# An audio tower in three phases: first layers of every batch, 32 experts as one line, last layers, with h and x kept in DRAM between them

## The reference

```python
hq = jnp.einsum('bqe,he->bqh', Q, W1q)          # 16 hidden features
hk = jnp.einsum('bke,he->bkh', K, W1k)
hid = jnp.tanh(hq[:, :, None, :] + hk[:, None, :, :] + b1)
est = jnp.einsum('bqkh,h->bqk', hid, W2[0]) + b2[0]
attn = jax.nn.softmax(scores + est, axis=-1)    # scores = Q K^T / sqrt(128)
return jnp.einsum('bqk,bke->bqe', attn, V)
```

## Time and profile before

| | |
|---|---|
| median of three runs | 5201.93 us (5199.91 to 5202.93) |
| the profiled execution's own time | 5203.53 us |
| its span, first to last instruction | 5201.7 us, 84447 instructions |
| TensorE busy | 4439.2 us, 85% of the span |
| ScalarE, VectorE, GpSimd busy | 2955.1, 2858.5, 705.4 us |
| mean granted TensorE clock | 0.910 |

### The profile page before, as it was taken

The page is one execution under the profiler, slowest core; times in us unless marked ns, Lnnn a source line. Parts: engine busy times, 40 slices in busy tenths (PEclk is TensorE's granted clock), DMA queues, the critical chain, the costliest instruction groups (busy, mean ns, idle before and its releaser), DMA issues.

```text
span 5201.7 us, 84447 instructions
## 1 busy us (share of the span) xinstructions
PE 4439.2 (85%) x24924; PEld 2449.2 (47%) x24924; DVE 2858.5 (55%) x6651; ACT 2955.1 (57%) x6370; POOL 705.4 (14%) x477
## 2 busy tenths in 40 slices
PE   4599997898659999789865999978985699997998
PEld 3344443466434444346643444434663344443566
DVE  5577773234457778223445777822344577772244
ACT  1177875754217777574421877856441277775644
POOL 0112221000021222100002122210000122221000
PEclk8699998999669999899966999989996699998999
DMA  2133320000113332000012333200001332320000
GB/s 92 20 46 49 54 34 32 3 27 9 52 23 44 47 54 34 32 8 22 11 49 28 42 45 54 34 32 9 21 13 48 37 42 42 47 34 32 13 17 16
DMA packets 97459, 175.25 MB, mean 34 GB/s; under 512 B 18400, under 2 KB 75152, under 8 KB 96272
## 3 DMA queue, kind: packets, MB, share of 16 engines
q1 hardware_dynamic: 97040, 170.00, 18.6%
HBM read 94.13 MB, written 1.53 MB: 18 GB/s over the span
## 4 chain that ended last, share of the span: by engine, by line
issue 49%; PE 43%; DVE 3%; POOL 1%; POOLq 1%; DMA 1%; DVEq 1%; ACT 1%; SPq 0%; ACTq 0%
PE ps L809 10%; PE ps L845 10%; PE ps L819 9%; PE ps L879 3%; PE ps L888 3%; PE ps L800 2%; PE ps L906 2%; DVE peaks L1548 2%; POOL rstd L545 1%; DMA k_stack<-parts 1%; PE ps L651 1%; PE ps L869 1%; PE ps L911 1%; DVE xn L1392 1%; PE ps L828 1%
## 5 line engine op out<-in xcount | busy, mean ns | idle before, releaser
L1548 DVE TENSOR_REDUCE peaks<-ps 128x1 f32<-128x748 f32 (+1 forms) x1536 | 1403.3, 933 | 505.1 <-PE ps L819 480.3
L1197 ACT ACTIVATE masked<-ps 128x384 f32<-128x384 f32 (+3 forms) x1536 | 679.8, 485 | 195.8 <-PE ps L809 181.9
L1197 ACT ACTIVATE probs<-ps 128x384 f32<-128x384 f32 (+1 forms) x1536 | 661.8, 484 | 93.7 <-PE ps L809 92.9
L545 POOL TENSOR_TENSOR rstd<-var,minus_half 128x6 f32<-128x6 f32 x104 | 138.3, 1330 | 3268.8 <-DVE var L1388 3268.8
L819 PE MATMUL ps<-k_stack,q_stack 96*128 96x374 bf16 (+1 forms) x1536 | 405.7, 349 | 113.8 <-DMA k_stack<-parts 87.4
L809 PE MATMUL ps<-shared 98*128 98x384 bf16 (+3 forms) x1536 | 440.1, 327 | 14.0 <-ACT probs L1197 6.8
L809 PE MATMUL ps<-q_stack,k_stack 98*128 98x384 bf16 (+3 forms) x1536 | 451.6, 330 | 0.5
L1449 DVE TENSOR_REDUCE top<-ps 128x1 f32<-128x128 f32 (+4 forms) x240 | 151.5, 631 | 426.2 <-PEq L715 354.1
L819 PE MATMUL ps<-shared 96*128 96x374 bf16 (+1 forms) x1536 | 372.2, 323 | 5.9 <-DVE peaks L1548 4.9
L1140 ACT ACTIVATE probs<-ps,neg_top 128x128 f32<-128x128 f32 (+4 forms) x240 | 152.9, 640 | 300.4 <-DVE neg_top L1457 246.8
L809 PEld LDWEIGHTS ps<-shared 98*128 98x128 bf16 (+1 forms) x1536 | 145.5, 103 | 353.4 <-ACT masked L1197 140.5
(11 more groups left out here) (276 smaller groups left out, 7794.3 us busy)
## 6 DMA issues: line engine op xcount, KB each, us to landing
shared<-parts SPq DMA_DIRECT2D x192, 187.0 KB, 9.2
wr<-in_l SPq DMA_DIRECT2D x32, 580.5 KB, 3.6
q_stack<-parts SPq DMA_DIRECT2D x96, 187.0 KB, 8.1
k_stack<-parts SPq DMA_DIRECT2D x96, 187.0 KB, 10.1
wts<-in_l SPq DMA_DIRECT2D x32, 514.5 KB, 3.5
shared<-in_tv SPq DMA_DIRECT2D x4, 4096.0 KB, 13.1
wrow<-in_l_rows SPq DMA_DIRECT2D x32, 320.0 KB, 4.1
wts<-in_l SPq DMA_DIRECT2D x32, 257.5 KB, 2.6
```

The lines of the kernel that those rows point to most:

```text
L545: pool.tensor_tensor(rstd[:, :], var[:, :], minus_half[:, :], ALU.pow).then_inc(S["rstd_ready"], 1)
L1197: act.activation(probs_ring(u)[0:m, 0:hi - lo], src[0:m, 0:hi - lo], ACT.Exp, scale=float(HD) ** -0.5).then_inc(S["ring_done"], 1)
L1548: v.tensor_reduce(peaks[0:m, g, j, head:head + 1], src[0:m, :, 0:T // 2], XY, ALU.max)\
```

## The change

The loop `batch` is split in three. The loop `front` does stages 1 and 2 for all four batches. Then one `experts()` without a loop does 32 experts as one pipeline (stages e = -1 to 32), those of batch 3 first (its xn, xT_, h and gates are still on the chip), then of batches 0, 1 and 2. The loop `tail` does stages 4 and 5 for all four. Between the phases h, xn, xT_ and the gates of a batch lie in DRAM tensors (`saved`): `spill` writes them at the end of each front, the pipeline loads those of the next batch in the midst of the last experts of the one before, `spill_merged` writes the merged h, and `load_hn` reads it for the tail into the new tile `hn`. The next x is loaded while the front before it still computes its gate; `tv` is loaded once. The store of the output is waited for only where h is written again (`out_free`).

In the additive attention the products of the projection weights are formed once at the start (`fold_ready`, `fold_done`: W1q Wq, W1k Wk, and Wk^T Wq), so that one set of products from xT_ gives the hidden parts and the scaled queries, and the keys are xT_ itself; hqb is made in two parts. The tanh ring has eight buffers in place of four. ScalarE's order is now tanh of tile u with the exponential of tile u - 1 after the fifth of them; the last tile has 14 tanh in place of 16. VectorE copies both halves of the turned probabilities. TensorE weighs tile u after the seventh tanh product of tile u + 2. ScalarE loads the table of exp at the head of a tail.

The diff, cut to its core:

```diff
+RUN = B * E
+STAGES = (B - 1,) + tuple(range(B - 1))
+def batch_of(x):
+    return STAGES[x // E]
+def first_of_stage(x):
+    return 0 < x < RUN and x % E == 0
...
-def additive_groups():
-    return [4 * (i % 4) + i // 4 for i in range(P // 8)]
+def additive_groups(u):
+    groups = min(P, T - u * P + 7) // 8
+    order = [4 * (i % 4) + i // 4 for i in range(P // 8)]
+    return [(g, g % 4 == 3 or g == groups - 1) for g in order if g < groups]
+ADDITIVE = [additive_groups(u) for u in range(NT)]
+AHEAD = 5
+BETWEEN = 7
+def tanh_order():
+    for u in range(NT):
+        for i, (g, _) in enumerate(ADDITIVE[u]):
+            yield "tanh", u, g
+            if u and i == AHEAD - 1:
+                yield "exp", u - 1, None
+    yield "exp", NT - 1, None
...
+            .rearrange("p (t d) -> p t d", t=NT)
+        saved = {name: nc.dram_tensor("saved_" + name, (B, P, width), F32).ap()
+                 for name, width in (("h", TP), ("xn", TP), ("xT", TP), ("gates", E * NT))}
...
-            return hid[:, i % 4, :] if i % 4 < 2 else masked[:, i % 4 - 2, :]
+            return (hid[:, 0, :], hid[:, 1, :], masked[:, 0, :], masked[:, 1, :], flat(x1), flat(att), flat(y),
+                    merged[:, 0:TP])[i % 8]
...
+            def spill(b, following=None):
+                sp.wait_ge(S["h_ready"], n.take("h_ready"))
+                sp.dma_start(saved["h"][b, :, :], flat(h)).then_inc(S["h_spilled"], 16)
+                if following is not None:
+                    load_x(following)
+                sp.wait_ge(S["front_done"], n.take("front_done"))
+                sp.dma_start(saved["xn"][b, :, :], flat(xn)).then_inc(S["front_spilled"], 16)
+                sp.dma_start(saved["xT"][b, :, :], xT_).then_inc(S["front_spilled"], 16)
+                sp.dma_start(saved["gates"][b, :, :], flat(gates)).then_inc(S["front_spilled"], 16)
+                sp.wait_ge(S["h_spilled"], n.take("h_spilled", 16))
+                sp.sem_inc(S["h_free"], 1)
+                sp.wait_ge(S["front_spilled"], n.take("front_spilled", 48))
+                sp.sem_inc(S["front_free"], 1)
+            def spill_merged(b):
+                sp.wait_ge(S["merged"], n.take("merged"))
+                sp.dma_start(saved["h"][b, :, :], flat(h)).then_inc(S["merged_spilled"], 16)
+                sp.wait_ge(S["merged_spilled"], n.take("merged_spilled", 16))
...
+                            if first_of_stage(x + 1):
+                                sp.dma_start(xT_, saved["xT"][batch_of(x + 1), :, :]).then_inc(S["xt_loaded"], 16)
+                            if first_of_stage(e - 1):
+                                spill_merged(batch_of(e - 2))
+                                sp.dma_start(flat(h), saved["h"][batch_of(e - 1), :, :]).then_inc(S["h_loaded"], 16)
+                                sp.dma_start(flat(gates), saved["gates"][batch_of(e - 1), :, :])\
+                                    .then_inc(S["h_loaded"], 16)
...
+                            if first_of_stage(e):
+                                sp.wait_ge(S["base_ready"], n.now("base_ready"))
+                                sp.dma_start(flat(xn), saved["xn"][batch_of(e), :, :]).then_inc(S["base_loaded"], 16)
...
-            with n.loop(sp, "batch", B, S["loop_entered"]) as b:
-                sp.wait_ge(S["x_free"], n.take("x_free"))
-                sp.dma_start(xT[:, 0:T_IN], A["xT"][b, :, :]).then_inc(S["x_loaded"], 16)
-                sp.dma_start(tv[:, :, :], A["tv"]).then_inc(S["tasks_loaded"], 16)
-                load_wq(0)
-                load_wr(0)
-                experts()
+            load_x(0)
+            sp.dma_start(tv[:, :, :], A["tv"]).then_inc(S["tasks_loaded"], 16)
+            load_wq(0)
+            load_wr(0)
+            with n.loop(sp, "front", B - 1, S["loop_entered"]) as b:
+                spill(b, b + 1)
+            spill(B - 1)
+            experts()
+            def tail(b, following=None):
...
+                    if stage == "l2" and following is not None:
+                        sp.wait_ge(S["hn_free"], n.take("hn_free"))
+                        load_hn(following)
...
+                sp.sem_inc(S["out_free"], 1)
+            spill_merged(STAGES[-1])
+            sp.sem_inc(S["out_free"], 1)
+            with n.loop(sp, "tail", B - 1, S["loop_entered"]) as b:
+                tail(b, b + 1)
+            tail(B - 1)
...
-            with n.loop(pool, "batch", B, S["loop_entered"]):
+            with n.loop(pool, "front", B, S["loop_entered"]):
                 power(6)
-                experts()
+            experts()
+            with n.loop(pool, "tail", B, S["loop_entered"]):
...
+            def additive_attention():
+                turns, width = {"tanh": 0}, T // 2
+                def scores(u, between=None):
+                    for a in range(2):
+                        pe.matmul(ps[:, 2 * (u % 2) + a, 0:width], tile_of(QT[:, 0, :], u),
+                                  xT_[:, a * width:(a + 1) * width], start=True, stop=False, skip_group_check=True)
+                    for i, (g, last) in enumerate(ADDITIVE[u]):
+                        if i == BETWEEN and between:
+                            between()
+                        pe.wait_ge(S["hidden_ready"], n.take("hidden_ready"))
+                        at = 32 * (g // 4)
...
+                    pe.drain().then_inc(S["scores_ready"], 1)
...
+                scores(0)
+                scores(1)
+                for u in range(NT):
+                    spread_out(u)
+                    if u + 2 < NT:
+                        scores(u + 2, lambda: weigh(u))
+                    else:
+                        weigh(u)
...
-            with n.loop(pe, "batch", B, S["loop_entered"]):
+            pe.transpose(ps[:, 0, 0:P], C("q2"), ident)
+            pe.transpose(ps[:, 0, P:2 * P], C("k2"), ident).then_inc(S["fold_ready"], 1)
+            pe.wait_ge(S["fold_done"], 1)
+            pe.matmul(ps[:, 1, 0:P], probs[:, 0, 0:P], C("hq2"), start=True, stop=True)
+            pe.matmul(ps[:, 1, P:2 * P], probs[:, 0, P:2 * P], C("hk2"), start=True, stop=True)
+            pe.matmul(ps[:, 1, 2 * P:3 * P], probs[:, 0, 0:P], probs[:, 0, P:2 * P], start=True, stop=True)\
+                .then_inc(S["fold_ready"], 1)
+            pe.wait_ge(S["fold_done"], 2)
+            with n.loop(pe, "front", B, S["loop_entered"]):
...
-                experts()
+            experts()
+            with n.loop(pe, "tail", B, S["loop_entered"]):
 
                 turn(xn)
-                feat([C("q2"), C("k2")], xT_, False)
...
-                feat([C("hq2")], QT[:, 0, :])
-                feat([C("hk2")], KT[:, 0, :])
-                pe.wait_ge(S["operand_ready"], n.take("operand_ready"))
-                attention(LAYER2, lambda u: tile_of(QT[:, 1, :], u), lambda u: KT[:, 0, :],
-                          lambda u, j: V[:, j, :], D)
+                additive_attention()
...
+            def additive_attention():
+                used = n.now("hidden_used")
+                i = 0
+                act.drain()
+                for what, u, g in tanh_order():
+                    if what == "exp":
+                        act.wait_ge(S["max_ready"], n.take("max_ready"))
+                        act.activation(cut(probs[:, u % 2, 0:T], T), scores_ap(u, T), ACT.Exp,
+                                       bias=neg_top[:, u % 2:u % 2 + 1], accum_out=total[:, u % 4:u % 4 + 1])\
+                            .then_inc(S["probs_ready"], 1)
+                        continue
+                    if g == 0 and u < 2:
+                        act.wait_ge(S["query_part_ready"], n.take("query_part_ready"))
+                    if i >= 8:
+                        act.wait_ge(S["hidden_used"], used + (i - 7))
+                    act.activation(tanh_ring(i)[:, 0:T], hid[:, 2, 0:T], ACT.Tanh,
+                                   bias=hqb[:, u * (P // 8) + g:u * (P // 8) + g + 1])\
+                        .then_inc(S["hidden_ready"], 1)
+                    i += 1
+                n.take("hidden_used", i)
...
+            with n.loop(act, "tail", B, S["loop_entered"]):
+                load_exp()
                 turned(xT_)
-                feat([(ACT.Copy, QT[:, 0, :], {}), (ACT.Copy, KT[:, 0, :], {})])
+                feat([(ACT.Identity, hid[:, 3, :], {"bias": C("b1_2")}), (ACT.Copy, hid[:, 2, :], {}),
+                      (ACT.Copy, QT[:, 0, :], {"scale": float(D) ** -0.5})])
...
+                def weighed(u):
+                    v.wait_ge(S["turned0"], n.take("turned0"))
+                    for half in range(2):
+                        v.tensor_copy(flat(probsT[:, 3 * half:3 * half + 3, :]), ps[:, 4 + half, 0:H0])\
+                            .then_inc(S["copied0"], 1)
+                    v.reciprocal(rtotal[:, u % 2:u % 2 + 1], total[:, u % 4:u % 4 + 1])
+                    v.drain()
+                    v.wait_ge(S["heads_ready"], n.take("heads_ready"))
```

(29 more changed lines are left out.)

171 lines of the change are left out of this document (93 added, 78 removed).

## The result

The changed kernel takes 4862.65 us (median of four runs, 4860.71 to 4868.15), the kernel before 5202.43 in the same comparison: ratio 0.9347, 95% interval 0.9331 to 0.9364. The profiled execution took 4862.37 us with a span of 4860.5. Predicted were 4856 us, in a range of 4822 to 4912.

The account below looks back on a forecast made before the run. TensorE was taken to bound the experts' midst, with time lost filling, draining and between batches, and ScalarE the additive attention. Terms summed to -346.3 us: 5203.5 becomes 4857.2 profiled, 4856 as median, range 4822 to 4912.

Parts of the forecast that it names:

- The likeliest case: Whole kernel: all terms come as summed, a median of 4856 us; chance 0.62.
- line of 32: Expert pipeline: of four fillings and drainings one stays, borders keep the 74.4 us pace; 222.6 us less.
- change of batch, fronts: Between successive fronts: x loaded early, no output store, TensorE's 13.9 us set the end; 7 us saved each, 21 less.
- heads of the tails: Start of each further tail: VectorE's jump back lies open, 1.5 us each, 4.5 us more.
- memsets once: Norm before the level 1 gate: GpSimd's memsets run once and slow it only once; 15.4 us less.
- last spill: After the last front: stores waited for before the stacks of expert 0 delay them; 6 us more, once.
- fold of the weights: Kernel start: forming the products of the weights beside the load of x costs 1 us more.
- additive attention: In each of four tails: earlier start and a tanh stream without waits save 24.7 us; 98.8 us less.
- the uneven line: Rival, expert pipeline: border transfers or a pace 1 us longer cost about 30 us, giving 4886 us; chance 0.12.
- The filling was work: Rival, expert pipeline: 28 us must be done at each border anyway, 84 us more, giving 4940; chance 0.04.
- The broken stream: Rival, additive attention: ScalarE still waits 3.6 us in each tile, 72 us more, giving 4928; chance 0.10.
- the slower rival: Rival, expert pipeline: 2.4 ms of busy TensorE lowers its granted clock, no faster than before; chance 0.03.

Follow-up runs that it names:

- experiment 2: The changed kernel with its line of 32 experts cut into four of 8, each filled and drained separately: 5091.6 us, ratio 0.9787.
- experiment 11: The changed kernel with both hardware loops over batches written out four times on all engines: 4846.8 us, ratio 0.9316.
- experiment 8: The changed kernel without the four stores of the last front's h, xn, xT_ and gates: 4856.3 us, ratio 0.9331.
- experiment 1: The kernel before, its batch loop kept, with only the new additive attention and its folded weights put in: 5103.2 us, ratio 0.9809.
- experiment 7: The changed kernel with GpSimd's three memsets also after each of the first three fronts, GpSimd's front loop written out: 4872.9 us, ratio 0.9363.
- experiment 5: The changed kernel with ScalarE's tanh allowed only four ahead of TensorE in place of eight: 4924.5 us, ratio 0.9463.

## Why the prediction was right, point by point

The likeliest case came, 6.7 us above its number. Term by term, in us:

| term | predicted | measured | from |
|---|---|---|---|
| line of 32 | -222.6 | -228.0 | experiment 2, three seams of 76 |
| change of batch, fronts | -21 | -19.0 | 3 x (23.0 - 16.6), means of three |
| heads of the tails | +4.5 | +9.8 | 3.41, 3.79 and 3.43 of issue, less the 0.29 each that experiment 11 leaves |
| memsets once | -15.4 | -15.3 | 3 x 5.1 by the rows; the run gave 10.2 |
| last spill | +6 | +3.7 | rows of experiment 8; its medians gave 6.4 |
| clock behind the stacks | 0 | +2.4 | in this execution; 155.85 - 153.48, cause open |
| fold of the weights | +1 | 0 | experiment 1 |
| additive attention | -98.8 | -100.5 | experiment 1 |
| within the fronts | 0 | +3.2 | 3 x 1.1, means of three, below |

The measured column sums to -343.7; between the two profiled executions lie 341.2 us. The sum can't be nearer than some 3 us, since it mixes medians with rows of single executions (experiment 1 has the spread of the first gate). That the forecast itself came within 6.7 us is partly luck: what it had too low (the heads by 5.3 us, the fronts within by 3.2, the changes of batch by 2.0) was nearly made up by what it had too high (the line by 5.4 us, the spill by 2.3).

*The line.* Right. The stages at the borders have the common pace, and the pace is 74.21 us, not 74.43, which makes a seam 1.7 us dearer. The transfers at the borders cost nothing, as said, and the uneven line is refuted with 12 us of room.

*The filling was work.* Refuted by experiment 2. In a seam TensorE's busy time is longer for the same products because the clock is low; once the line runs through, that time isn't owed.

*The change of batch among the fronts.* The size was right (19 us, in the range of 16 to 25), the reason half wrong. I let TensorE's 13.9 us set the end and laid ScalarE's 2.76 us of issue on it. TensorE jumps for next to nothing; VectorE is the one that stands still, for 4.0 to 4.2 us, and keeps h's first tiles from TensorE's fifth. h itself was free at about the time I gave. TensorE sets the end, as I had it, only when VectorE's jump is gone (experiment 11).

*The heads of the tails.* This is the term that was mis-sized: 1.5 us each with a bound of 2.8, measured 3.4 to 3.8. I took ScalarE's row as the bound for VectorE. ScalarE itself takes 2.7 to 2.9 us at the three heads of after, as in the kernel before, but 0.17 us at a change of fronts, where VectorE takes 4.0 to 4.2; a turn of a front has some 80 instructions on ScalarE, 300 on VectorE and 410 products on TensorE, a turn of a tail 460 and 505 on the first two. The section on instruction fetch in the Trainium skill's page "Runtime: NRT & Kernel Launch" says that a taken branch outside the prefetch window stalls for a fetch; the trace agrees, on VectorE in both loops and on ScalarE in the long one, and experiment 11 takes VectorE's stall away. The rule gives no price, and on TensorE no stall is to be seen.

*Memsets.* Right to a tenth by the rows. In experiment 7 a third of the memsets' cost is missing from the run, spread over steps of 0.3 to 0.8 us within a front. Steps of that kind are in all of these kernels: from the last statistics of h to the end of the gate, without the slow norm's 5.1 us, the last three fronts of after take 157.1 to 157.3 us, two of the unrolled kernel 155.4 and 155.5, those of experiment 7 155.7, and the three of before 155.7, 158.0 and 154.9. They move with each edit, in before from turn to turn too, and with no one operation. Where they come from stays open; that GpSimd's jump is the cause was tried and is wrong.

*The last spill.* The mechanism was right and the size too high: the stacks start 3.75 us after the end of the gate, where I had 5.5, and the first maxima come 26.2 us after the gate's last operation begins, 4.0 more than the 22.2 of the earlier trace rows and not the 6 that I gave as a sign. That experiment 8 gave 6.4 is luck.

*Additive attention.* Right. The start saved 6.66 us (first projection to first tanh 6.80 in place of 13.46), which is the 6.9 of a clock that rises midway, not the 5.5 that I took. The body took 88.97 us against 88.4; the end, from the last tanh to the last addition, 8.5 against 7.6. The broken stream, the rival that I gave 0.10, exists: experiment 5 has it, at 62 us, with four buffers. My argument against it (eight buffers, TensorE bound by ScalarE) held for six as well.

*The clock.* It stands at 1.00 in the windows view from 820 us to 3120, and at 0.98 as a mean from the line's first row maxima on, 2.4 ms of TensorE at 97% busy, so the slower rival did nothing; the Trainium skill's rule that the prediction weighed against it, from "TensorE: Matmul & The Clock Gate" (Seeing it yourself), agrees with that. The lower clock is found at the change of batch (0.50) and behind the wait for the stacks (0.55).

## What to carry to other kernels

When a pipeline is drained and filled at every turn of an outer loop, price the seam as its length less the paces in it, and count its low clock as part of the price: here that was 76 us a turn, and storing and loading a batch's state took it away, for 3.7 us at the last front and nothing to be seen at the borders. Before a ring is called long enough, take the consumer's whole absence, with the way there and back, and not the work alone that it does meanwhile. And a jump back costs on each engine for itself; it shows as issue without a releaser, and where code space allows, writing the outer loop out removes it. Before a small step of the clock is put down to an edit, look for it in the other kernels' traces: what looked like the spill's doing here is absent from seven kernels that have the spill.

## What the runs showed of the hardware

- A jump back over a front or a tail costs VectorE 3.4 to 4.2 us of issue. ScalarE takes 2.7 to 2.9 at the tails and 0.17 at the fronts, and TensorE nothing beyond what it waits for anyway. Writing out two loops of four turns saved 15.8 us.
- One GpSimd memset of two partitions (12288 elements in all, 5.21 us) holds back a VectorE norm of 1.63 us until it is done: 6.7 us. It doesn't touch a copy out of PSUM that starts 1.1 us into it (0.56 us, as elsewhere).
- From the first product behind the stacks to the first gate column pass 153.3 to 153.5 us or 155.8 to 155.9, with a clock of 0.60 or 0.55 in the first 33.7 us. Kernels that waited 25.4 to 25.6 us before it are found in both groups.
